# A state-space convolution in front of two gated feed-forward layers: the first quarter prepared in another order

## The chip, the core and the metric

One Trainium2 chip, one core. The time is the device time of one execution in microseconds. The kernel before was run three times: 1150.04, 1151.3 and 1151.69 us, median 1151.3 us. The profile is of a fourth execution.

## The reference

`x` is 64 rows of 32 heads by 512 positions, float32. All of it is computed in one launch:

```python
K = 2.0 * einsum('hn,hnl->hl', Ct, exp(dtA[:, :, None] * arange(512))).real   # a 512-tap filter for each of 32 heads
y = causal_convolution(x, K) + x * D[:, None]        # written with an FFT of length 1024
y = y * (arange(512) < length[batch])                # a mask by the length of the row
x1 = x + FFN0(y)        # w2(silu(w1 y) * (w3 y)), width 1792, weights scaled by blocks of 128 x 128
x2 = x1 + FFN1(x1)      # width 1376, with a low-rank term per batch row, gathered by index
out = x2 + gelu(BitLinear(x2))      # RMS norm, 8-bit activations, ternary weights
```

The filter needs, for each head, sines, cosines and powers of 64 complex numbers; `K` comes out of small products of two tables, S (16 coarse steps) and Fm (32 fine steps).

## The kernel before

**Tiling.** The 32 heads are worked in four quarters of eight (`NT`, `HPT`), 512 tokens each (64 rows by 8 heads). A quarter is at once a tile of the first feed-forward layer. Products are fp32 in three passes: each operand is split into a rounded high part and a low remainder, and `mm3` (lines 137 to 139) issues high x high, high x low and low x high. The high part is always written by ScalarE (a copy with rounding), the low part by VectorE (a subtraction that needs the high part).

**A filter on its way to TensorE.** For quarter t: `angles(t)` makes the arguments of the sines in `theta`, four operations on 128 x 512, in place, by GpSimd; `sines(t)` on ScalarE fills one of two `trig` buffers; `magnitudes(t)` on GpSimd fills one of two `mag` buffers by nine doublings, once VectorE has the powers `pw`; `state_tables(t)` on VectorE makes S, Fm and a small term `dm` for `D`; `state_sums(t)` on TensorE makes the filter in a PSUM bank `pk`; `kernel_high(t)` and `kernel_low(t)` split it; SP writes both halves to DRAM rows (`kernel_rows`) and reads them back as Toeplitz blocks (`toeplitz`), 128 shifted copies of each row, in four pairs of heads, two loads of 512 KB for each pair (high and low).

**Convolution and chunk.** `conv(t)` multiplies for each pair q the Toeplitz blocks with x, 24 products of 64 to 256 columns, in turn into two PSUM banks; VectorE masks (line 1298), ScalarE rounds (`conv_high`), VectorE subtracts (`low_half`, line 1288). The result stands where x stood in `a_hi`, `a_lo` and is the input of the feed-forward layer. `chunk(c)` is two blocks of 128 hidden units for all four tiles: for each tile twelve gate and twelve up products of 512 columns for block 0, the same for block 1, then 24 down products. In chunk 0 the convolution of tile t + 1 is put between up and down products of tile t. The up products of block 1 reuse the bank that the silu of block 0 has read (`pe.wait_ge(s_silu[0], m + 1)`).

**Order.** Each engine has its instructions written out in order, and semaphores tie the engines together. Nothing is reordered: an instruction that waits holds all behind it on its engine, DMA issues on SP too. ScalarE's order in the front is: two small sines, `sines(0)`, `x_high(0)`, `sines(1)`, `kernel_high(0)`, `sines(2)`, `kernel_high(1)`, `sines(3)`, first weights, `conv_high(0)`, `x_high(1)`, chunk 0. VectorE: `exp32` for the step sizes (14 operations), the step itself, `exp32` for the powers (a multiplication and 14 operations on 128 x 288), coefficients, `state_tables` 0 and 1, `kernel_low(0)`, `x_low(0)`, `kernel_low(1)`, the mask, scaling of the first weights (line 1271), `masked(0)` with the low halves of these weights (`first_weights`) after pairs 0 and 1, `x_low(1)`, `state_tables` 2 and 3, chunk 0. GpSimd: `angles(0)`, four small ones for `den`, `angles(1)`, `magnitudes` 0 and 1, then `angles` and `magnitudes` of 2 and of 3, masks and an identity. A `link` makes the next VectorE (or GpSimd) instruction wait for the end of the one before. TensorE: `state_sums` 0 and 1, `conv(0)`, chunk 0 with `state_sums` 2 and 3 ahead of `conv(1)`. SP: parameters (three loads), x tile 0 and small inputs, first weights, zeros, `kernel_rows(0)`, `toeplitz(0)`, x tile 1, `kernel_rows(1)`, `toeplitz(1)` (each pair waits until `conv(0)` has read the buffer), x tiles 2 and 3, weights, indices, quarters 2 and 3.

## Time and profile before

| | us |
|---|---|
| median of three runs | 1151.3 |
| profiled execution, its own time | 1152.8 |
| its span, first to last instruction | 1150.9 |
| TensorE in products | 1067.7 (93%) |
| TensorE loading weights | 900.1 (78%) |
| VectorE | 548.8 (48%) |
| ScalarE | 302.9 (26%) |
| GpSimd | 154.8 (13%) |

The engines' busy shares by slices of 1/40 of the span, 28.8 us each, in tenths; PEclk is the granted clock of TensorE:

```
PE   0799999999999999999889999999999999988774
DVE  7544554334344444344763343443443343357786
ACT  1222221211212121211441121122132131124675
POOL 7800000000000000000141001001010010023425
PEclk9999999999999999999999999999999999998897
DMA  2775310010101000020311022021021021032103
```

TensorE does nothing of weight in the first slice, is filled from the third on, and thins out in the last four. GpSimd is busy only in the first two slices. The granted clock is written as a share of 2.4 GHz; where it is 0.5, the array runs at 1.2 GHz. PE is TensorE, PEld its weight loads, DVE VectorE, ACT ScalarE, POOL GpSimd, SPq the queue on which SP issues DMAs.

### The profile page before, as it was taken

Reading aid. Unit: us, or ns where it says so; the run is one execution under the profiler, and the core shown is the slowest. Engines: PE = TensorE matmul, PEld = TensorE weight load, DVE = VectorE, ACT = ScalarE, POOL = GpSimd, SP = SyncE. Lnnn points to the kernel's source line nnn. Section 1 sums busy time; section 2 is a strip of 40 time slices with the busy share of each in tenths; the row PEclk is TensorE's granted clock in tenths of the full one; section 3 lists DMA queues with packets and bytes.
Section 4 is the critical chain, followed back from the end, with each engine's and each line's share of the span. In section 5 each row is a group of like instructions: output and inputs, shape, how many; then the busy total and the mean of one; then the engine's idle time right before and its main releaser. Section 6 shows DMA issues by size and latency. Waiting matters only on the chain.

```text
span 1150.9 us, 13707 instructions
## 1 busy us (share of the span) xinstructions
PE 1067.7 (93%) x5431; PEld 900.1 (78%) x5434; DVE 548.8 (48%) x661; ACT 302.9 (26%) x485; POOL 154.8 (13%) x194
## 2 busy tenths in 40 slices
PE   0799999999999999999889999999999999988774
PEld 0679888888888888888778888888888888876651
DVE  7544554334344444344763343443443343357786
ACT  1222221211212121211441121122132131124675
POOL 7800000000000000000141001001010010023425
PEclk9999999999999999999999999999999999998897
DMA  2775310010101000020311022021021021032103
GB/s 100 236 247 197 111 41 16 1 55 0 55 0 55 0 15 39 0 92 1 128 65 54 30 68 68 27 82 55 27 84 53 27 97 39 27 110 74 47 1 146
DMA packets 26655, 73.92 MB, mean 64 GB/s; under 512 B 5442, under 2 KB 5634, under 8 KB 26498
## 3 DMA queue, kind: packets, MB, share of 16 engines
q1 hardware_dynamic: 20994, 48.35, 12.0%
q0 software_dynamic: 5632, 25.17, 7.1%
q8 instruction: 19, 0.31, 0.1%
q14 instruction: 10, 0.08, 0.0%
HBM read 69.15 MB, written 4.36 MB: 64 GB/s over the span
## 4 chain that ended last, share of the span: by engine, by line
PE 84%; DVE 5%; POOL 4%; issue 3%; ACT 2%; DMA 1%; SPq 0%; DVEq 0%; ACTq 0%; POOLq 0%
PE ps_gu L137 18%; PE ps_gu L138 18%; PE ps_gu L139 18%; PE ps_d L137 8%; PE ps_d L138 8%; PE ps_d L139 8%; PE ps_t L139 1%; PE ps_t L138 1%; PE ps_t L137 1%; POOL theta L435 1%; POOL mag L435 1%; DMA lr_raw<-in_tab_l,rows 1%; PE ps_gu L836 1%; PE ps_t L727 1%; POOL trig L431 1%
## 5 line engine op out<-in xcount | busy, mean ns | idle before, releaser
L137 PE MATMUL ps_gu<-a_hi,gu_hi 128*128 128x512 f32 x800 | 316.4, 396 | 2.2 <-DVE a_lo L1288 2.2
L138 PE MATMUL ps_gu<-a_lo,gu_hi 128*128 128x512 f32 x800 | 313.9, 392 | 0.0
L139 PE MATMUL ps_gu<-a_hi,gu_lo 128*128 128x512 f32 x800 | 313.1, 391 | 0.0
L139 PEld LDWEIGHTS ps_gu<-a_hi,gu_lo 128*128 128x128 f32 x800 | 151.2, 189 | 32.5
L137 PEld LDWEIGHTS ps_gu<-a_hi,gu_hi 128*128 128x128 f32 x800 | 151.9, 190 | 31.5 <-DVE a_lo L1288 2.3
L138 PEld LDWEIGHTS ps_gu<-a_lo,gu_hi 128*128 128x128 f32 x800 | 151.8, 190 | 28.6
L1425 DVE TENSOR_TENSOR s_act<-s_act,ps_gu 128x512 f32<-128x512 f32 x44 | 30.2, 687 | 194.7 <-PE ps_gu L139 194.6
L1318 DVE TENSOR_TENSOR s_act<-s_act,ps_gu 128x512 f32<-128x512 f32 x56 | 38.5, 687 | 152.8 <-PE ps_gu L139 152.8
L307 POOL DMA_INDIRECT lr_raw<-in_tab_l,rows x48 | 46.0, 959 | 369.3 <-PE ps_t L727 345.4
L137 PE MATMUL ps_d<-h_hi,dn_hi 128*128 128x512 f32 x224 | 87.6, 391 | 0.0
L139 PE MATMUL ps_d<-h_hi,dn_lo 128*128 128x512 f32 x224 | 87.2, 389 | 0.0
L138 PE MATMUL ps_d<-h_lo,dn_hi 128*128 128x512 f32 x224 | 87.2, 389 | 0.0
L932 ACT ACTIVATE s_act<-ps_gu 128x512 f32<-128x512 f32 x56 | 33.5, 598 | 183.5 <-PE ps_gu L139 183.4
L1364 DVE TENSOR_TENSOR acc<-acc,ps_d 128x2048 f32<-128x2048 f32 x24 | 54.9, 2287 | 48.5 <-PE ps_d L139 48.4
L936 ACT ACTIVATE h_hi<-s_act 128x512 fp32r<-128x512 f32 x56 | 35.4, 632 | 158.2 <-DVE s_act L1318 158.2
L307 POOL DMA_INDIRECT ar_raw<-in_tab_a,rows x8 | 8.1, 1016 | 489.9 <-PE ps_d L139 409.2
L1005 ACT ACTIVATE s_act<-ps_gu 128x512 f32<-128x512 f32 x44 | 26.3, 598 | 176.8 <-PE ps_gu L139 176.8
L137 PE MATMUL ps_d<-dn_hi,h_hi 128*128 128x512 f32 x176 | 68.8, 391 | 0.2 <-DVE x1b L1529 0.2
L138 PE MATMUL ps_d<-dn_lo,h_hi 128*128 128x512 f32 x176 | 68.7, 391 | 0.0
L139 PE MATMUL ps_d<-dn_hi,h_lo 128*128 128x512 f32 x176 | 68.5, 389 | 0.0
L1011 ACT ACTIVATE h_hi<-s_act 128x512 fp32r<-128x512 f32 x44 | 27.8, 631 | 151.3 <-DVE s_act L1425 149.9
L1471 DVE TENSOR_TENSOR x1b<-x1b,ps_d 128x2048 f32<-128x2048 f32 x20 | 45.7, 2287 | 36.3 <-PE ps_d L139 36.3
(239 smaller groups left out, 1727.6 us busy)
## 6 DMA issues: line engine op xcount, KB each, us to landing
raw<-in_w SPq DMA_DIRECT2D x26, 768.0 KB, 5.7
toep_hi<-krev_hi SPq DMA_DIRECT2D x16, 512.0 KB, 5.9
toep_lo<-krev_lo SPq DMA_DIRECT2D x16, 512.0 KB, 6.9
acc<-in_x_t SPq DMA_DIRECT2D x4, 1024.0 KB, 10.1
out<-x1b SPq DMA_DIRECT2D x16, 256.0 KB, 2.0
w_all<-in_wq SPq DMA_DIRECT2D x1, 1024.0 KB, 8.3
raw<-in_wq SPq DMA_DIRECT2D x4, 256.0 KB, 4.3
lr_raw<-in_tab_l,rows POOLq DMA_INDIRECT x48, 4.1
```

The lines of the kernel that those rows point to most:

```text
L137: pe.matmul(out_ap, st_hi, mv_hi, start=start, stop=False, skip_group_check=skip)
L138: pe.matmul(out_ap, st_hi, mv_lo, start=False, stop=False, skip_group_check=skip)
L139: return pe.matmul(out_ap, st_lo, mv_hi, start=False, stop=stop, skip_group_check=skip)
L307: return pool.indirect_dma_start(out=dst, out_offset=None, in_=table, in_offset=bass.IndirectOffsetOnAxis(ap=group, axis=0))
L932: act.activation(s_act[:, f], ps_gu[G_BANK[f]], ACT.Silu).then_inc(s_silu[f], 1)
L936: act.activation(h_hi[:, f], s_act[:, f], ACT.Copy).then_inc(s_hh[f], 1)
L1005: act.activation(s_act[:, f], ps_gu[G_BANK[f]], ACT.Silu).then_inc(s_silu[f], 1)
L1011: act.activation(h_hi[:, f], s_act[:, f], ACT.Copy).then_inc(s_hh[f], 1)
L1318: dve.tensor_tensor(s_act[:, f], s_act[:, f], ps_gu[U_BANK[f]], ALU.mult).then_inc(s_mul[f], 1)
L1364: dve.tensor_tensor(x_tile(acc, t), x_tile(acc, t), ps_d[:], ALU.add).then_inc(s_ev, 1)
L1425: dve.tensor_tensor(s_act[:, f], s_act[:, f], ps_gu[U_BANK[f]], ALU.mult).then_inc(s_mul[f], 1)
L1471: dve.tensor_tensor(zt, zt, ps_d[:], ALU.add).then_inc(s_ev, 1)
```

## The change

- **Angles.** `angles(t)` moves from GpSimd to VectorE. `angles(0)` stands ahead of the powers, `angles(1)` behind `state_tables(0)` and `x_low(0)`, `angles(2)`, `x_low(1)` and `angles(3)` behind all of the first convolution's work, ahead of `state_tables` 2 and 3. GpSimd keeps the magnitudes, now in one row. The argument of the angles (`turns`) and the powers have places of their own.
- **Parameters.** The load of the step sizes and decays is issued first, and `exp32` waits for it alone.
- **First Toeplitz rows.** The filter of quarter 0 is copied unsplit (`k_f`), written once and loaded once, four loads of 512 KB in place of eight; ScalarE rounds each pair of heads on chip and VectorE subtracts in place (`first_toeplitz_low`), 128 x 1024 each. Loads of the later quarters are as before.
- **State sums.** Those of quarter 1 stand before pair 2 of `conv(0)`, those of quarters 2 and 3 before pairs 2 and 3 of `conv(1)`, and the halves of these filters are made between the masks of that convolution.
- **Filling products.** Fourteen products of 512 columns on `a_hi` stand before `conv(0)`, once the filter of quarter 0 has landed in DRAM. They write a PSUM bank that nobody reads before it is written anew.
- **ScalarE and VectorE** have their work of the front in another order, written out in the diff; `sines(2)` and `sines(3)` now stand between `x_high(1)` and the first silu.

Line numbers of the diff are those of the listing above; indentation is cut and "..." marks what is left out.

```diff
@@ -40,6 +40,7 @@
+BUSY = 14
@@ -311,9 +315,9 @@
-    sp.dma_start(e3[:, 2], par[:, 2]).then_inc(s_par, 16)
...
-    sp.dma_start(par_sb[:, 2:4], par[:, 3:5]).then_inc(s_par, 16)
+    sp.dma_start(e3[:, 2], par[:, 2]).then_inc(s_par2, 16)
+    sp.dma_start(par_sb[:, 2:4], par[:, 3:5]).then_inc(s_par2, 16)
@@ -329,23 +333,31 @@
-            sp.wait_ge(s_half, t + 1)
+            sp.wait_ge(s_half, t)
...
+    def first_toeplitz():
+        sp.wait_ge(s_kf, 1)
+        sp.dma_start(krev[0][0:HPT, 0:L].rearrange("h (a b) -> a h b", b=NB), k_f[:]).then_inc(s_kw[0], 16)
+        sp.wait_ge(s_kw[0], 16)
+        sp.wait_ge(s_kz, 32)
+        for q in range(4):
+            sp.dma_start(toep_lo[:, 2 * q:2 * q + 2].bitcast(F32),
+                         bass.AP(tensor=krev[0].tensor, offset=2 * q * KROW,
+                                 ap=[[1, P], [KROW, 2], [1, L]])).then_inc(s_T[q], 16)
...
-            if t:
-                sp.wait_ge(s_conv, 4 * (t - 1) + q + 1)
+            sp.wait_ge(s_conv, 4 * (t - 1) + q + 1)
...
-    kernel_rows(0)
-    sp.wait_ge(s_kz, 32)
-    toeplitz(0)
+    first_toeplitz()
@@ -427,28 +439,11 @@
-    def ts(o, i, a, b, op0, op1=None):
-        link(pool.tensor_scalar(o, i, a, b, op0, op1) if op1 is not None
-             else pool.tensor_scalar(o, i, a, 0.0, op0, ALU.add))
...
-    r0, den, d2 = sm[3][:], sm[4][:], sm[5][:]
-    def angles(t):
-        hs = slice(t * HPT, (t + 1) * HPT)
-        if t:
-            pool.wait_ge(s_trig, t)
-        if t >= 2:
-            pool.wait_ge(s_sf, 3 * (t - 1))
-        rnd = trig[:, t % 2]
-        tt(theta[:], bc(r0[:, hs], 2, 64), bc(lgrid[:], 1, HPT), ALU.mult)
-        tt(theta[:], theta[:], bc(shift[:], 1, HPT), ALU.add)
-        ts(rnd, theta[:], MAGIC, MAGIC, ALU.add, ALU.subtract)
-        pool.tensor_tensor(theta[:], theta[:], rnd, ALU.subtract).then_inc(s_theta, 1)
+    den, d2 = sm[4][:], sm[5][:]
@@ -465,17 +460,12 @@
-    angles(0)
...
-    angles(1)
...
-    magnitudes(0)
-    magnitudes(1)
-    for t in range(2, NT):
-        angles(t)
+    for t in range(NT):
@@ -585,12 +575,26 @@
+    def busy_array():
+        pe.wait_ge(s_xh, 1)
+        pe.wait_ge(s_kw[0], 16)
+        for k in range(BUSY):
+            pe.matmul(ps_gu[0], a_hi[:, k % KB, 0:P], a_hi[:, k % KB, 0:TT], start=True, stop=True)
...
-            pe.wait_ge(s_T[q], 32 * (t + 1))
+            if t == 0 and q == 2:
+                state_sums(1)
+            if t == 1 and q >= 2:
+                state_sums(q)
+            if t:
+                pe.wait_ge(s_T[q], 32 * t + 16)
+            else:
+                pe.wait_ge(s_tl, q + 1)
@@ -630,13 +634,10 @@
                 last.then_inc(s_u[f], 1)
-            if first and t == 0:
-                for n in range(2, NT):
-                    state_sums(n)
             if first and t + 1 < NT:
...
             if first and t == 0:
-                pe.wait_ge(s_kl, NT)
+                pe.wait_ge(s_kl, NT - 1)
             for f in range(2):
@@ -665,7 +666,7 @@
     state_sums(0)
-    state_sums(1)
+    busy_array()
     conv(0)
@@ -893,34 +894,37 @@
         act.wait_ge(s_kp, t + 1)
-        if t >= 2:
-            act.wait_ge(s_kw[t - 2], 32)
+        if t == 3:
+            act.wait_ge(s_kw[1], 32)
         act.activation(k_hi[:, t % 2], pk[:, t], ACT.Copy).then_inc(s_kh, 1)
+    def conv_high(t, pairs=(0, 1, 2, 3)):
+        for q in pairs:
+            h0 = t * HPT + 2 * q
+            act.wait_ge(s_cmul, 4 * t + q + 1)
+            act.activation(a_hi4[:, :, h0:h0 + 2].rearrange("p k h b -> p h k b"),
+                           ytmp[:, q % 2].rearrange("p h (k b) -> p h k b", k=KB), ACT.Copy).then_inc(s_yhi, 1)
...
     sines(1)
-    kernel_high(0)
-    sines(2)
-    kernel_high(1)
-    sines(3)
+    act.wait_ge(s_kp, 1)
+    act.activation(k_f[:], pk[:, 0], ACT.Copy).then_inc(s_kf, 1)
     for f in range(2):
...
                        raw[:, f, 0:2].rearrange("p a n -> p (a n)"), ACT.Copy).then_inc(s_whg[f], 1)
+        for q in (2 * f, 2 * f + 1):
+            act.wait_ge(s_T[q], 16)
+            act.activation(toep_hi[:, 2 * q:2 * q + 2], toep_lo[:, 2 * q:2 * q + 2].bitcast(F32),
+                           ACT.Copy).then_inc(s_th, 1)
         act.activation(dn_hi[:, f], raw[:, f, 2], ACT.Copy).then_inc(s_whd[f], 1)
-    def conv_high(t):
-        for q in range(4):
-            h0 = t * HPT + 2 * q
-            act.wait_ge(s_cmul, 4 * t + q + 1)
-            act.activation(a_hi4[:, :, h0:h0 + 2].rearrange("p k h b -> p h k b"),
-                           ytmp[:, q % 2].rearrange("p h (k b) -> p h k b", k=KB), ACT.Copy).then_inc(s_yhi, 1)
-    conv_high(0)
+    conv_high(0, (0,))
+    kernel_high(1)
+    conv_high(0, (1, 2, 3))
     x_high(1)
-    act.wait_ge(s_mag, NT)
+    sines(2)
+    sines(3)
@@ -943,9 +947,12 @@
+                conv_high(1, (0,))
...
+                conv_high(1, (1,))
...
-            if first and t + 1 < NT:
+                conv_high(1, (2, 3))
+            elif first and t + 1 < NT:
@@ -1186,18 +1193,36 @@
-    dve.wait_ge(s_par, 48)
+    dve.wait_ge(s_par, 16)
...
-    ar, ai, ut, r0, den, d2, em, t0 = (t[:] for t in sm)
+    ar, ai, ut, _, den, d2, em, t0 = (t[:] for t in sm)
+    r0 = turns[:]
...
+    dve.wait_ge(s_par2, 32)
...
+    def angles(t):
+        hs = slice(t * HPT, (t + 1) * HPT)
+        rnd = trig[:, t % 2]
+        if t:
+            dve.wait_ge(s_trig, t)
+        if t >= 2:
+            dve.wait_ge(s_sf, 3 * (t - 1))
+        tt(theta[:], bc(r0[:, hs], 2, 64), bc(lgrid[:], 1, HPT), ALU.mult)
+        tt(theta[:], theta[:], bc(shift[:], 1, HPT), ALU.add)
+        ts(rnd, theta[:], MAGIC, MAGIC, ALU.add, ALU.subtract)
+        dve.tensor_tensor(theta[:], theta[:], rnd, ALU.subtract).then_inc(s_theta, 1)
...
+    dve.wait_ge(s_plink, 2)
+    dve.wait_ge(s_step, 1)
+    angles(0)
@@ -1240,9 +1265,9 @@
-        dve.wait_ge(s_kh, t + 1)
-        if t >= 2:
-            dve.wait_ge(s_kw[t - 2], 32)
+        dve.wait_ge(s_kh, t)
+        if t == 3:
+            dve.wait_ge(s_kw[1], 32)
@@ -1253,29 +1278,28 @@
-    state_tables(0)
-    state_tables(1)
-    kernel_low(0)
-    x_low(0)
-    kernel_low(1)
-    dve.wait_ge(s_len, 16)
-    link(dve.tensor_copy(len_f[:], len_i[:]))
-    dve.wait_ge(s_grid, 3)
-    link(dve.tensor_tensor(cmask[:], pos[:], bc(len_f[:], 1, KB), ALU.is_lt))
-    dve.wait_ge(s_sc0, 16)
-    for f in range(2):
+    def first_scale(f):
...
-    def first_weights(f):
+    def first_toeplitz_low(q):
+        dve.wait_ge(s_th, q + 1)
+        pair = toep_lo[:, 2 * q:2 * q + 2]
+        dve.tensor_tensor(pair, pair.bitcast(F32), toep_hi[:, 2 * q:2 * q + 2].bitcast(F32),
+                          ALU.subtract).then_inc(s_tl, 1)
+    def first_gate_up_low(f):
...
+    def first_down_low(f):
@@ -1288,19 +1312,24 @@
+    def mask(t, q):
+        j = 4 * t + q
+        dve.wait_ge(s_conv, j + 1)
+        if j >= 2:
+            dve.wait_ge(s_yhi, j - 1)
+            dve.wait_ge(s_ylo, j - 1)
+        dve.tensor_tensor(ytmp[:, q % 2], conv_bank[q % 2].rearrange("p (i n) -> p i n", i=2),
+                          bc(cmask[:].rearrange("p k b -> p (k b)"), 1, 2), ALU.mult).then_inc(s_cmul, 1)
...
-            dve.wait_ge(s_conv, 4 * t + q + 1)
-            if 4 * t + q >= 2:
-                dve.wait_ge(s_yhi, 4 * t + q - 1)
-                dve.wait_ge(s_ylo, 4 * t + q - 1)
-            dve.tensor_tensor(ytmp[:, q % 2], conv_bank[q % 2].rearrange("p (i n) -> p i n", i=2),
-                              bc(cmask[:].rearrange("p k b -> p (k b)"), 1, 2), ALU.mult).then_inc(s_cmul, 1)
+            mask(t, q)
...
-            if t == 0 and q < 2:
-                first_weights(q)
+            if t == 1 and q in (1, 2):
+                kernel_low(q + 1)
@@ -1326,9 +1355,6 @@
-            if first and t == 0:
-                kernel_low(2)
-                kernel_low(3)
@@ -1368,8 +1394,37 @@
-    masked(0)
+    state_tables(0)
+    x_low(0)
+    angles(1)
+    dve.wait_ge(s_len, 16)
+    link(dve.tensor_copy(len_f[:], len_i[:]))
+    dve.wait_ge(s_grid, 3)
+    link(dve.tensor_tensor(cmask[:], pos[:], bc(len_f[:], 1, KB), ALU.is_lt))
+    dve.wait_ge(s_sc0, 16)
+    first_scale(0)
+    first_toeplitz_low(0)
+    state_tables(1)
+    first_toeplitz_low(1)
+    first_scale(1)
+    first_gate_up_low(0)
+    mask(0, 0)
+    first_toeplitz_low(2)
+    mask(0, 1)
+    first_toeplitz_low(3)
+    low_half(0, 0)
+    kernel_low(1)
+    first_gate_up_low(1)
+    mask(0, 2)
+    low_half(0, 1)
+    mask(0, 3)
+    low_half(0, 2)
+    low_half(0, 3)
+    for f in range(2):
+        first_down_low(f)
+    angles(2)
...
+    angles(3)
...
```

## Rows read from the trace of the kernel before

**Rows 1.** The page, the chain that ended last: shares of the span by engine.

```profile
PE 84%; DVE 5%; POOL 4%; issue 3%; ACT 2%; DMA 1%; SPq 0%; DVEq 0%; ACTq 0%; POOLq 0%
```

**Rows 2.** Waits of TensorE, 0 to 130 us: total us, times, longest us.

```profile
PE ps_d L582 <- DVE Fm L1239: 28.9, 2, 27.1
PE ps_t L137 <- DMA toep_lo<-krev_lo: 5.6, 1, 5.6
```

**Rows 3.** Timeline, 0 to 60 us: start, duration, engine, line, operation, tiles, [idle before].

```profile
3.50 0.20 DVE L1165 TENSOR_SCALAR tmp<-par_sb 128x64 f32<-128x64 f32 x1 [3.50 <-DMA par_sb<-in_par]
...
7.96 1.30 DVE L1169 TENSOR_TENSOR pin<-sm,pow 128x288 f32<-128x288 f32 x1
...
11.28 0.31 DVE L1166 TENSOR_SCALAR tmp<-tmp 128x288 f32<-128x288 f32 x1
...
19.22 0.46 DVE L1172 SCALAR_TENSOR_TENSOR pw<-tmp,kint 128x288 f32<-128x288 f32 x1
...
21.87 3.25 POOL L435 TENSOR_TENSOR mag<-mag,pw 128x8 f32<-128x8 f32 x9
...
25.11 0.62 DVE L1169 TENSOR_TENSOR S<-coef,trig 128x128 f32<-128x128 f32 x2
...
29.14 0.37 ACT L898 ACTIVATE k_hi<-ps_d 16x256 fp32r<-16x256 f32 x1 [6.79 <-PE ps_d L584]
...
32.75 0.39 SPq L342 DMA_DIRECT2D toep_hi<-krev_hi  x1
...
38.46 0.55 PE L137 MATMUL ps_t<-a_hi,toep_hi 128*128 128x256 f32 x1 [5.62 <-DMA toep_lo<-krev_lo]
```

**Rows 4.** DMA issues, 28 to 33 us: size, median us from issue to landing.

```profile
krev_lo<-k_lo SPq DMA_DIRECT2D x1, 16.0 KB, 1.5
```

**Rows 5.** Loads of toep_hi, 28 to 52 us.

```profile
DMA to landing us min/median/max: 3.7/6.4/10.0
```

**Rows 6.** VectorE by shape, 0 to 80 us: busy us, mean ns | idle before.

```profile
L1251 DVE TENSOR_TENSOR a_lo<-acc,a_hi 128x2048 fp32r<-128x2048 f32 x2 | 4.6, 2282 | 1.1 <-ACT a_hi L891 1.1
L1271 DVE TENSOR_TENSOR raw<-raw,scale 128x1536 f32<-128x1536 f32 x2 | 3.4, 1763 | 0.0
L1288 DVE TENSOR_TENSOR a_lo<-ytmp,a_hi 128x512 fp32r<-128x512 f32 x4 | 2.8, 688 | 0.1
L1276 DVE TENSOR_TENSOR gu_lo<-raw,gu_hi 128x1024 fp32r<-128x1024 f32 x2 | 2.5, 1251 | 7.0 <-ACT gu_hi L909 7.0
```

**Rows 7.** ScalarE by shape, 0 to 80 us.

```profile
L909 ACT ACTIVATE gu_hi<-raw 128x1024 fp32r<-128x1024 f32 x2 | 2.1, 1040 | 0.0
...
L932 ACT ACT_TABLE_LOAD x1 | 1.3, 1283 | 4.4 <-PE ps_gu L139 4.4
```

**Rows 8.** Timeline, 60 to 140 us.

```profile
61.66 0.80 PE L137 MATMUL ps_gu<-a_hi,gu_hi 128*128 128x512 f32 x1 [2.17 <-DVE a_lo L1288]
...
66.89 0.39 PE L137 MATMUL ps_gu<-a_hi,gu_hi 128*128 128x512 f32 x1
...
77.34 0.39 PE L137 MATMUL ps_t<-a_hi,toep_hi 128*128 128x256 f32 x1
...
80.08 0.37 PE L137 MATMUL ps_gu<-a_hi,toep_hi 128*128 128x256 f32 x1
```

**Rows 9.** Windows, TensorE: us, busy (products), granted clock, DMA share, GB/s.

```profile
38.50:59.00 20.50, 20.32 (x95) 1.00 0.83 283
1037.36:1045.36 8.00, 8.00 (x33) 0.65 0.21 66
...
1093.91:1101.91 8.00, 6.53 (x37) 0.79 0.00 0
```

**Rows 10.** Timeline of TensorE, 1020 to 1151 us.

```profile
1050.72 0.50 PE L137 MATMUL ps_d<-gu_hi,h_hi 128*128 128x512 f32 x1 [2.67 <-DVE h_lo L1571]
...
1093.91 0.56 PE L137 MATMUL ps_d<-gu_hi,h_hi 128*128 128x512 f32 x1 [2.83 <-DVE h_lo L1571]
```

More of the change, by code:

```diff
@@ L103, in build @@
             pin = sb("pin", [P, 9, HEADS])
-            pw = sb("pw", [P, 9, HEADS])
             tmp = [sb(f"tmp{i}", [P, 9 * HEADS]) for i in range(4)]
@@ L145, in build @@
         s_par, s_drow, s_len, s_ix, s_rb, s_id = (sem(n) for n in ("s_par", "s_drow", "s_len", "s_ix", "s_rb", "s_id"))
+        s_par2, s_kf, s_th, s_tl = (sem(n) for n in ("s_par2", "s_kf", "s_th", "s_tl"))
         r_row, r_next = sem("r_row"), sem("r_next")
@@ L201, in build @@
             coef = [sb(f"coef{i}", [P, HEADS]) for i in range(2)]
+            turns = sb("turns", [P, HEADS])
+            pw = sb("pw", [P, 9, HEADS])
+            k_f = sb("k_f", [NA, HPT, NB])
             drow = sb("drow", [1, HEADS])
@@ L877, in _ @@
                 act.wait_ge(s_step, 1)
-                act.activation(trig_small[0], sm[3][:], ACT.Sin, scale=TWO_PI).then_inc(s_sin, 1)
-                act.activation(trig_small[1], sm[3][:], ACT.Sin, scale=TWO_PI / 2).then_inc(s_sin, 1)
+                act.activation(trig_small[0], turns[:], ACT.Sin, scale=TWO_PI).then_inc(s_sin, 1)
+                act.activation(trig_small[1], turns[:], ACT.Sin, scale=TWO_PI / 2).then_inc(s_sin, 1)
                 def sines(t):
```

## The prediction

> **What bounds the kernel now.** I read the page's shares of the ending chain first: TensorE holds 84% of it, so a change counts only by what it takes out of TensorE's own sequence or out of the time before that sequence closes up [rows 1]. Second, TensorE's waits in the first 130 us: 27.1 us until the first state tables, 5.6 us for Toeplitz rows [rows 2], and 2.17 us before the first gate product [rows 8]. All of the change lies there; behind 62 us the order of TensorE's work is only rearranged by a few microseconds and I let it shift as a block. Third, the timeline of the first 60 us, for the path that ends these waits: parameters at 3.50, powers of the decay written by 19.7, tables from 25.11, kernel rows rounded at 29.14, first Toeplitz DMA issued at 32.75, first convolution product at 38.46 [rows 3].
>
> Fourth, the clock. Convolution products run from 38.5 to 59 at 20.32/95 = 0.214 us each [rows 9], in the next quarter at (80.08 - 77.34)/24 = 0.114 us [rows 8]. The first twelve gate products take 5.23 us from 61.66 to 66.89, 0.436 each, and the one at 66.89 is the first short one [rows 8]. The granted clock reads 1.00 in the front all the same, while a later stretch of 8 us with the same slow start reads 0.65: 1.2 GHz for 0.35 x 2 x 8 = 5.6 us, then 2.4 [rows 9]. I read the front column as not yet recording and go by the spacing: everything before 66.7 is at 1.2 GHz, as the products there are spaced, though TensorE was in products without a break from 38.5 to 59. Dense 512-column products bring the rise (5.0 and 5.6 us after their start, 3.4 in a third place [rows 9]), the convolution's mix of short ones does not; once risen, the mix keeps it. So the change is worth what it does to the start of the chunk and to the clock of 96 convolution products.
>
> **Start to first Toeplitz row.** The first vector work, at 3.50 [rows 3], now waits for the first of three loads instead of the last: a gain between nothing and half of the 3.50; I take 0.8, an estimate. Angles for quarter 0 go on VectorE ahead of the powers: three operations of two tensors at 0.69 (L1288 has their size [rows 6]) and one scalar operation, between 0.31 (288 columns [rows 3]) and 0.69, I take 0.45; with the links 2.5 us. The powers then run without GpSimd beside them: before, 7.96 to 19.68 = 11.7 us, with the first multiplication at 1.30 [rows 3]. Alone, 10 operations at 0.46 + 0.03 and 5 at 0.31 + 0.03 are 6.6 us (bounds 6.6 and 11.7; the two rows at 0.46 and 0.31 are what they cost with GpSimd quiet). Powers at 16.3 instead of 19.7. GpSimd's nine multiplications, 3.25 us, then end near 19.9, before they are wanted at 21.5. Coefficients lay between 19.68 and 25.11 [rows 3]; one of them stood against GpSimd, I take 4.4 for 5.4. Tables from 20.7, kernel sums ready 4.0 later as before (25.11 to 29.14): 24.7. Of the 4.0 the last 2.0 are the sums, as TensorE waited until 27.1 [rows 2].
>
> Now comes a new wait. ScalarE has the second sines ahead of the rounding of the kernel row, VectorE has x_low(0) (2.28 [rows 6]) and four angle operations (2.5) behind the tables that end at 22.5. The sines finish at 28.0 rather than when the sums are ready at 24.7, and the copy k_f ends at 28.4. One DMA write instead of two and no low half: 1.5 us for such a write [rows 4]; I take 1.7, between 1.5 and 2.2, rows issued at 30.1 against 32.75. Both x_low(0) and the angles now run beside GpSimd's magnitudes, nine operations in 3.25 us [rows 3]. Between nothing and one of these, 0.36 us, in front of each of five vector operations is 0 to 1.8 us; I take 0.5: issue at 30.6. The page "SBUF — State Buffer" of the Trainium skill (section "SBUF: two separate sides") says that a VectorE operation with two SBUF inputs and a GpSimd operation that reads SBUF take one port pair by exclusive lock, the loser waiting for a whole instruction. The rows agree where they show it (1.30 against 0.46 above), and by the rule all five would wait. That is the rule that speaks against this change: by it the rows are issued at 31.9 and the time is 1.3 us above mine.
>
> Of the Toeplitz loads the quickest landed 3.7 us after its issue and the slowest 10.0 [rows 5]. That is 6.3/7 = 0.9 between neighbours beside the 0.5 between their issues (0.39 for one [rows 3] and a gap), so four loads land at 34.3, 35.7, 37.1, 38.5. ScalarE rounds one in 1.04, VectorE subtracts in 1.25 [rows 7, 6]: convolution pair 0 at 36.7 against 38.46.
>
> **Filling products.** They start when the kernel row has landed, 30.6, and 14 at 0.43 are 6.0 us: over by 36.6, just before pair 0, so they cost nothing; each microsecond by which the Toeplitz rows came sooner, or the kernel row later, would show as loss, up to the whole 6.0. If the rise comes 3.4 to 5.6 us after their start it comes inside them. Value: pairs at 2.74 instead of 5.13.
>
> **Convolution of quarter 0, warm.** Now VectorE paces it, with the table of quarter 1 and the second scaling in its queue. From pair 0 at 36.7: tables(1) 1.7 (they lie in the 2.0 between 25.11 and 27.1), low(1) 1.25, pair 1 at 39.6; scaling 1.76, gate low 1.25, mask 0.69, low(2) 1.25 (ScalarE's gate rounding 1.04 and rounding of pairs 2 and 3 lie under it but for 0.3), mask, low(3) 1.25 [rows 6, 7]. Pair 2 starts at 44.6, pair 3 follows at 47.3 and ends at 50.2; mask, rounding and low half cost 2.17 as before [rows 8]: gate products at 52.4 against 61.66, gain 9.3. The state sums of quarter 1 (half of 2.0 at the fast clock) fall into the 2.3 us hole between pairs 1 and 2. SP's loads for quarter 1 wait for kernel_low(1), behind low(3) and a low half on VectorE: out at 47.5, written at 49, eight loads landed by 63, wanted from 66. The x tiles and weights behind them on SP, 3.5 MB at 283 GB/s [rows 9], land by 76, and none is wanted before 80.
>
> **First chunk.** Twelve warm products take 2.9, not 5.2: 2.3 more. Against that stands a second new wait. The first silu must come before the fourth product group, at 52.4 + 8.3 = 60.7. ScalarE has sines(2) and sines(3) ahead of it, these wait for VectorE: two down lows at 0.69, angles 2.5, x_low(1) 2.28, angles 2.5; then sine 0.6 (half of 1.04 for 1024 columns, and a start), table load 1.28 [rows 7], silu 0.6: 52.4 + 11.1 = 63.5. TensorE stands 2.8 us. Bounds: 0 if the sums above are 2.8 too long, 4 if each operation meets one more delay. In the kernel before ScalarE waited for the gate product before that load, with products running, so it cost nothing. State sums 2 and 3 change place, 2.2 us either way; their kernel_high and kernel_low sit between masks and need nothing on time.
>
> **Sum.** 9.3 + 2.3 - 2.8 = 8.8 us. The profiled execution took 1152.8 with a span of 1150.9; the median of three is 1151.3, and the difference is taken off that: **1142.5**.
>
> **The clock in the new holes.** A hole of 2.67 us left TensorE at 2.4 GHz, one of 2.83 us was followed by a slow stretch of 0.21 x 2 x 8 = 3.4 us [rows 9, 10]. The silu hole is 2.8 by launch and 2.6 by records, on that edge. If the clock falls there, the fourth group runs slow and the rise comes within it or just behind it: 1.7 to 3.4 us more, inside my likeliest case. The page "TensorE: Matmul & The Clock Gate" of the Trainium skill (section "Why this matters for your kernels") allows holes up to about 3 us between bursts, by which this hole is harmless and the sum stays 8.8; the row with 2.83 us goes against it, so I don't rely on it.
>
> **Rivals.** (A) *The filling does not raise the clock.* For it: the rise needed up to 5.6 us, and the filling offers 6.0 with a gap behind it; 20 us of convolution did not raise it. Against it: all three known rises fit in. Then pairs stay at 5.13: end of pair 3 at 36.7 + 4 x 5.13 + 2.1 for the sums = 59.3, against 61.66 - 2.17 = 59.5, chunk slow start as before, silu late by about 0.5: **1151.3** within 1. (B) *The clock rises and falls in the 2.3 us before pair 2*, where only state sums run. Two pairs at 5.13 cost 4.8, the slow start of the chunk is then hidden in the silu hole: **1147.3**. For it: the convolution mix is thin on both sides. Against: 2.3 is below 2.67. (C) *Slower:* the silu hole drops the clock and the fourth group is too short to bring it back (12 x 0.427 = 5.1 us, known rises 3.4 to 5.6), so the convolution of quarter 1 runs slow as quarter 0 did: 12 x 0.2 + 96 x 0.1 + 2 for the sums + 2.4 in the down products = 16.4. 1142.5 + 16.4 = **1158.9**. It decides as soon as the hole passes 2.7 to 2.8 and the rise takes over 5.1 us. (D) *Port conflicts eat the front:* the full 1.8 instead of 0.5 and powers at 9 us instead of 6.6 give 1146, still faster.
>
> **Chances.** Likeliest case 0.67 (own range 1139.5 to 1146.5, with D), B 0.10, A 0.13, C 0.07, others 0.03. The range from 1139 to 1149.5 holds the first two and the near edge of others; it leaves out A and C. A measurement can tell about 0.2%, 2.3 us, from no change. Faster 0.80, within 0.2% 0.12, slower 0.08.
>
> **What would show it.** k_f's copy right behind the second sines near 28.5 and not behind the sums; products of 0.23 us spacing by the end of the filling; convolution pairs of 2.74; first gate product near 52.4 with 0.23 spacing from the start; a hole near 60.7 to 63.5 ended by silu; the whole order of TensorE 8.8 earlier from the first down product on. The forecast is wrong if the filling ends at 0.43, if pairs 2 and 3 start more than 2 us off, or if slow products follow the hole at 60.7 for more than 4 us.

## The result, and the profile after

The changed kernel takes 1146.72 us (median of 14 runs, 1142.74 to 1151.06) against 1151.59 for the kernel before (14 runs, 1150.04 to 1153.90): a ratio of 0.995, interval 0.9938 to 0.9962. The forecast was 1142.5 with a range of 1139 to 1149.5. The profiled run took 1143.93 us with a span of 1142.1, that is 8.9 less than the profiled run of before (1152.82).

The 14 runs are not one heap. Six lie between 1142.7 and 1143.9 with a mean granted clock of 0.984 to 0.987; six between 1147.7 and 1148.9 with 0.977 or 0.978; one stands between them (1145.7, 0.983) and one above (1151.1, 0.975). The kernel before shows no such groups in its 14 runs. So the median of 1146.7 stands in a gap between two groups, and the profile is of the quicker one. What makes the other is a question of its own below.

The shares of the ending chain in the page of after, against [rows 1]; the waits of TensorE from 0 to 130 us (total, times, longest), against [rows 2]:

```profile
PE 84%; DVE 8%; ACT 3%; issue 2%; DMA 2%; POOL 1%; DVEq 0%; ACTq 0%; POOLq 0%
```

```profile
PE ps_d L572 <- DVE Fm L1264: 23.2, 1, 23.2
PE ps_gu L583 <- DMA krev_hi<-k_f: 5.2, 1, 5.2
PE ps_gu L137 <- ACT s_act L936: 2.6, 1, 2.6
PE ps_gu L137 <- DVE a_lo L1312: 2.2, 1, 2.2
PE ps_t L137 <- DVE toep_lo L1291: 2.2, 2, 1.3
```

The timeline of after from 0 to 90 us (start, duration, engine, line, operation, tiles, [idle before]), against [rows 3, 8]:

```profile
2.56 0.20 DVE L1172 TENSOR_SCALAR tmp<-par_sb 128x64 f32<-128x64 f32 x1 [2.56 <-DMA par_sb<-in_par]
...
15.74 0.46 DVE L1179 SCALAR_TENSOR_TENSOR pw<-tmp,kint 128x288 f32<-128x288 f32 x1
...
16.56 3.16 POOL L443 TENSOR_TENSOR mag<-mag,pw 128x8 f32<-128x8 f32 x9
...
20.11 5.93 POOL L443 TENSOR_TENSOR mag<-mag,pw 128x8 f32<-128x8 f32 x9
...
22.67 0.41 DVE L1264 TENSOR_TENSOR Fm<-trig,mag 128x256 f32<-128x256 f32 x1
23.00 2.27 DVE L1276 TENSOR_TENSOR a_lo<-acc,a_hi 128x2048 fp32r<-128x2048 f32 x1
...
28.36 0.36 ACT L912 ACTIVATE k_f<-ps_d 16x256 f32<-16x256 f32 x1
...
30.29 1.92 SPq L346 DMA_DIRECT2D toep_lo<-krev_hi  x4
...
30.40 5.06 PE L583 MATMUL ps_gu<-a_hi 128*128 128x512 f32 x14 [5.21 <-DMA krev_hi<-k_f]
...
36.74 0.36 PE L137 MATMUL ps_t<-a_hi,toep_hi 128*128 128x256 f32 x1 [1.28 <-DVE toep_lo L1291]
...
44.32 0.39 PE L137 MATMUL ps_t<-a_hi,toep_hi 128*128 128x256 f32 x1 [0.89 <-DVE toep_lo L1291]
...
52.13 0.50 PE L137 MATMUL ps_gu<-a_hi,gu_hi 128*128 128x512 f32 x1 [2.17 <-DVE a_lo L1312]
...
61.19 1.28 ACT L936 ACT_TABLE_LOAD   x1
62.48 0.60 ACT L936 ACTIVATE s_act<-ps_gu 128x512 f32<-128x512 f32 x1
...
63.13 0.50 PE L137 MATMUL ps_gu<-a_hi,gu_hi 128*128 128x512 f32 x1 [2.57 <-ACT s_act L936]
...
86.58 2.29 DVE L1390 TENSOR_TENSOR acc<-acc,ps_d 128x2048 f32<-128x2048 f32 x1
```

Windows of TensorE in after (us, busy and products, granted clock, DMA share, GB/s), against [rows 9]. The record of the clock starts with its first change, so 1.00 ahead of that says nothing; in the last two rows it does:

```profile
36.74:39.45 2.71, 2.71 (x24) 1.00 1.06 404
...
63.13:64.50 1.37, 1.36 (x6) 1.00 1.05 386
64.50:68.00 3.50, 3.50 (x12) 0.51 1.07 403
```

What the reader is to see: the fourteen fill products take 5.06 us where fourteen at 0.43 would take 6.0, so the clock rises inside them; a convolution pair then takes 2.71 instead of 5.13, and the gate products start at 52.13 instead of 61.66 [rows 8]. Behind the hole of 2.57 us that the silu leaves, the clock is at 1.2 GHz for 3.5 us. One landmark holds the whole front together, the first accumulation on VectorE: 86.58 here, and in the kernel before

```profile
94.01 2.29 DVE L1364 TENSOR_TENSOR acc<-acc,ps_d 128x2048 f32<-128x2048 f32 x1
```

so 7.4 of the 8.9 us come from ahead of it, and 1.5 from slow stretches further on that lie elsewhere from run to run: in the trace of before the granted clock is 0.50 from 561.8 to 565.1 us with 17 products, in that of after it is 1.00 there.

### The profile page after: what moved, and what is told of

Its sections match the earlier page's. It is cut to its first block, busy times and chain, and to the rows that moved or that the text cites. A ratio compares the mean times of both kernels' runs of the same rounds, so it can differ in the third digit from the quotient of the medians.

```text
span 1142.1 us, 13740 instructions
## 1 busy us (share of the span) xinstructions
PE 1059.2 (93%) x5448; PEld 891.6 (78%) x5448; DVE 556.2 (49%) x680; ACT 306.7 (27%) x489; POOL 135.7 (12%) x178
## 4 chain that ended last, share of the span: by engine, by line
PE 84%; DVE 8%; ACT 3%; issue 2%; DMA 2%; POOL 1%; DVEq 0%; ACTq 0%; POOLq 0%
PE ps_gu L137 18%; PE ps_gu L138 18%; PE ps_gu L139 18%; PE ps_d L137 8%; PE ps_d L138 8%; PE ps_d L139 8%; PE ps_t L139 1%; PE ps_t L137 1%; PE ps_t L138 1%; DMA lr_raw<-in_tab_l,rows 1%; PE ps_gu L837 1%; PE ps_t L728 1%; DVE ar_lo L1443 1%; DVE z_new L1576 1%; ACT a_hi L1001 1%
## 5 line engine op out<-in xcount | busy, mean ns | idle before, releaser
L1018 ACT ACTIVATE h_hi<-s_act 128x512 fp32r<-128x512 f32 x44 | 27.8, 631 | 151.6 <-DVE s_act L1480 150.2
```

Source lines behind the costliest of these rows:

```text
L1018: act.activation(h_hi[:, f], s_act[:, f], ACT.Copy).then_inc(s_hh[f], 1)
```

## The experiments

The theory: the gain is the clock's, raised by the filling and kept by the convolution; the rearranged front only makes room for it. The rivals: the front's own microseconds count; the filling is needed in part only; the second group of runs comes from somewhere else than the front.

| kernel | median us (runs) | ratio to before, interval | first gate product | first accumulation |
|---|---|---|---|---|
| before | 1151.6 (14) | | 61.66 | 94.01 |
| after | 1146.7 (14) | 0.995, 0.9938 to 0.9962 | 52.13 | 86.58 |
| after again | 1144.3 (6) | 0.994, 0.9921 to 0.996 | 51.90 | 84.78 |
| after, third time | 1143.8 (5) | 0.9933, 0.992 to 0.9947 | 52.24 | 86.70 |
| no filling | 1152.2 (12) | 1.0003, 0.9994 to 1.0013 | 61.44 | 94.33 |
| 8 fill products | 1152.8 (11) | 1.0006, 0.9996 to 1.0015 | 61.41 | 94.32 |
| filling alone | 1152.1 (11) | 1.0002, 0.9992 to 1.0011 | 61.67 | 93.65 |
| ScalarE queue alone | 1151.6 (11) | 0.9998, 0.9989 to 1.0007 | 61.44 | 92.78 |
| filling and ScalarE queue | 1143.4 (5) | 0.9923, 0.9909 to 0.9937 | 54.41 | 85.72 |
| bridged hole | 1143.2 (6) | 0.9925, 0.9909 to 0.994 | 51.78 | 84.68 |
| silu sooner | 1146.4 (6) | 0.9946, 0.9925 to 0.9968 | 56.01 | 87.48 |
| reordered | 1138.2 (4) | 0.9875, 0.986 to 0.989 | 50.27 | 81.92 |
| reordered again | 1139.7 (5) | 0.9898, 0.9883 to 0.9914 | 50.49 | 81.21 |
| reordered and bridged | 1139.9 (4) | 0.9887, 0.9872 to 0.9902 | 50.25 | 80.93 |

Each ratio is to the kernel before as it ran beside that kernel (medians 1151.6 to 1152.2 us). Both repeats, no filling, the bridged hole, silu sooner and "reordered again" ran on one chip (number 9), the other experiments on another (number 6). The last two columns are of the profiled run alone. One run of the filling alone took 6057 us, for no reason that a trace shows; the medians don't feel it.

**The same kernel again, twice.** No edit.

> The changed kernel once more, for the spread of its runs and for a second trace. So far its runs fall into two groups, about 1143.4 and 1148.3 us, with one at 1151, and the profiled one is of the first group: there the clock rose within the filling products and stayed up through the first convolution. Theory: in the slower group the clock falls in the hole between convolution pairs 1 and 2 (only state sums there), pairs 2 and 3 run at 5.1 us instead of 2.7, and the gate products start near 57 instead of 52.1. Rival: in the slower group the filling products do not raise the clock at all; then all four pairs run at 5.1 us and the time is 1151. Rival: the clock falls only in the hole before the first silu and stays down through the second convolution; that would cost 10 us and more, and the runs would stand at 1153 or above. Expected: median between 1143 and 1148.5, both groups present.

> The changed kernel once more, for its second group of runs. Of 20 runs so far 11 lay at 1142.6 to 1145.7 with a mean clock of 0.983 to 0.988, nine at 1147.7 to 1151.1 with 0.975 to 0.978. If the second group is the clock fallen in the hole before pair 2, any profile with a mean of 0.978 shows pairs 2 and 3 at 5.1 and gate products near 56.3, and every run with 0.978 lies 4.5 to 5 us above those with 0.985; a profile with 0.985 shows them at 2.74 and 52.1. If it is something else (falls in the tail), the front is the same in both.

The runs of the first repeat: 1142.6, 1143.9, 1142.6, 1144.6 (clock 0.984 to 0.988) and 1147.9, 1148.1 (0.978). Of the second: 1142.6 to 1143.8 three times, 1145.2 and 1145.8 with 0.981 and 0.979. Over all 25 runs of this kernel nine lie at 1147.7 or above. On this chip it is two in 11, and five runs in a row without one. No profile fell into that group, so the last expectation was not decided for it; its other half held, the profile with 0.987 shows the gate products at 52.24. The first repeat's profile shows another fall, behind the hole ahead of the gate products:

```profile
51.90:53.00 1.10, 1.10 (x5) 1.00 1.01 268
53.00:57.00 4.00, 4.00 (x12) 0.57 1.03 347
57.00:61.00 4.00, 4.00 (x19) 1.00 1.05 401
```

It costs nothing: the silu comes when ScalarE is through, and TensorE then waits 0.95 us for it instead of 2.57. In that trace the clock is then spared behind the silu hole, and the first accumulation comes at 84.78.

**No filling.** The call of `busy_array` removed.

```
                 state_sums(0)
-                busy_array()
                 conv(0)
```

> The changed kernel without the fourteen filling products. If the clock is what the change gains, all four pairs of the first convolution run slow (5.1 us each), gate products start near 61.5 as in the kernel before, the wait for the first silu shrinks to about 0.5 us, and the time is 1151 to 1152, equal to the kernel before. If the rearranged front itself gained, it would be 1149 or less.

TensorE's rows of that kernel:

```profile
36.54 0.55 PE L137 MATMUL ps_t<-a_hi,toep_hi 128*128 128x256 f32 x1 [11.48 <-DVE toep_lo L1290]
46.90 1.03 PE L572 MATMUL ps_d<-dm,onehot 1*16 1x256 f32 x2
...
61.44 0.80 PE L137 MATMUL ps_gu<-a_hi,gu_hi 128*128 128x512 f32 x1 [2.17 <-DVE a_lo L1311]
```

Pair 0 starts 1.9 us sooner than before [rows 3], two pairs take 10.36 us as before, the state sums between them eat the 1.9 (2.0 us at the slow clock), and the gate products start where they always did. The rearranged front without the clock is worth nothing.

**Eight fill products.** `BUSY = 8`.

> The changed kernel with 8 filling products instead of 14: they end near 33.8, and TensorE stands some 2.9 us before pair 0. If the rise needs the filling up to pair 0, all four pairs run at 5.13 and the time is 1151 to 1152, as without filling. If 3.4 us are enough and the gap does no harm, 1143 to 1144. If it is a matter of where the rise happens to fall, runs of one kernel scatter between 1143 and 1152, and the median lies between.

```profile
PE ps_t L137 <- DVE toep_lo L1291: 2.7, 1, 2.7
```

```profile
36.92:38.00 1.08, 1.08 (x7) 0.72 1.06 412
38.00:59.20 21.20, 21.20 (x109) 0.50 0.46 144
```

First the wait ahead of pair 0, then two windows. In this trace the clock did rise, since a fall is recorded in pair 0: the rise is lost behind a hole of 2.7 us ahead of the convolution, and the convolution didn't bring it back in 21 us. None of eleven runs was below 1151.1. Eight of them have a mean clock of 0.971 to 0.974, three have 0.986, the value of the kernel before, whose front is not in the record: in these three the filling probably raised nothing; they took 1152.4 to 1153.4. Fourteen products, with a hole of 1.28 behind them, kept it: here the filling had to come closer to the convolution.

**The filling alone**, in the kernel before, with nothing rearranged.

```
+                def busy_array():
+
+                    pe.wait_ge(s_xh, 1)
+                    pe.wait_ge(s_kw[0], 32)
+                    for k in range(BUSY):
+                        pe.matmul(ps_gu[0], a_hi[:, k % KB, 0:P], a_hi[:, k % KB, 0:TT], start=True, stop=True)
...
                 state_sums(1)
+                busy_array()
                 conv(0)
```

> The kernel before with the fourteen filling products alone, between the state sums of quarter 1 and pair 0, released when both kernel rows of quarter 0 have landed; nothing of the front is rearranged. If the gain is the clock's alone: fill from about 32.5 to 38.5, pair 0 at 38.6, four pairs at 2.74 without the split on VectorE between them, gate products near 51.8 instead of 61.66, warm from the start, 1140 to 1144, as good as the whole change. If the rearranged front is needed for it (the 1.9 us by which pair 0 comes sooner, and the sums in another place), 1145 to 1148. If the clock doesn't rise here, 1151.6.

Neither of the first two came: the clock rose (fourteen products in 4.60 us), and yet nothing was gained. The timeline of that kernel, four engines:

```profile
38.60 0.36 PE L138 MATMUL ps_t<-a_hi,toep_hi 128*128 128x256 f32 x1 [1.21 <-DMA toep_lo<-krev_lo]
...
48.65 1.26 POOL L452 TENSOR_TENSOR theta<-theta,trig 128x512 f32<-128x512 f32 x1
...
49.95 0.63 ACT L895 ACTIVATE trig<-theta 128x512 f32<-128x512 f32 x1 [11.20 <-POOL theta L452]
50.48 1.04 ACT L918 ACTIVATE gu_hi<-raw 128x1024 fp32r<-128x1024 f32 x1
...
51.55 1.28 DVE L1285 TENSOR_TENSOR gu_lo<-raw,gu_hi 128x1024 fp32r<-128x1024 f32 x1 [7.52 <-ACT gu_hi L918]
...
53.37 0.68 DVE L1307 TENSOR_TENSOR ytmp<-ps_gu,cmask 128x512 f32<-128x512 f32 x1
...
54.20 0.55 PE L138 MATMUL ps_gu<-a_hi,toep_hi 128*128 128x256 f32 x1 [6.76 <-DVE ytmp L1307]
```

```profile
54.20:59.30 5.10, 5.10 (x24) 0.50 1.02 308
```

Read it upwards from the last product, the first of pair 3 (the expectation of the next experiment calls it pair 2): TensorE waits for a bank that the mask has to empty; the mask stands in VectorE's queue behind the low half of the weights; that waits for ScalarE's rounding; and that stands in ScalarE's queue behind the sines of quarter 3, whose angles GpSimd delivers at 49.9. The kernel before has the same chain (its VectorE idles 7.0 us for `gu_hi` [rows 6]), but there slow products cover it, and the same product comes at the same time behind a wait of 0.18 us:

```profile
54.19 0.55 PE L137 MATMUL ps_gu<-a_hi,toep_hi 128*128 128x256 f32 x1 [0.18 <-DVE ytmp L1298]
```

With quick products it becomes a hole of 6.8 us, and behind the hole pair 3 runs at the slow clock.

**ScalarE's queue, with and without the filling.** Everything else as in the kernel before:

```
                 kernel_high(0)
-                sines(2)
                 kernel_high(1)
-                sines(3)
                 for f in range(2):
...
+                sines(2)
                 conv_high(0)
                 x_high(1)
+                sines(3)
                 act.wait_ge(s_mag, NT)
```

> The kernel before with two edits: the fourteen filling products, and on ScalarE the roundings of kernel row 1 and of the weights ahead of the sines of quarters 2 and 3, which wait for GpSimd. Nothing else of the front is rearranged. In the trace of the filling alone the clock rose, but ScalarE stood for the angles of quarter 3 until 49.95 with the weight rounding queued behind it, VectorE stood behind that rounding with the masks of pairs 1 to 3 behind it, and TensorE stood 6.8 us before pair 2. If that queue is the whole reason why the filling alone gave nothing: pair 0 at 38.6, no hole above 1 us until the convolution ends near 49.8, gate products near 51.9 to 52.5, no silu hole (sines of quarter 3 are done by 53), first accumulation at 82 to 83 instead of 94.0, total 1139.5 to 1142: better than the changed kernel. If the rest of the rearranged front is needed as well (GpSimd's share, split on chip), 1145 or more.

> The kernel before with the reordered ScalarE queue and without filling. By both theories no gain: the convolution of quarter 0 stays at 5.13 per pair (no dense products before it) and sets the gate products near 61.5; 1151 to 1152. If it gains over 1 us, ScalarE's queue cost time on its own in the kernel before, and part of any gain of the two edits together is that.

The order alone gives nothing, the filling alone nothing, both together 8.7 us by their medians: as much as the quicker group of the changed kernel, with the front left alone. The total was 1.4 us above the upper end that I had given, the gate products 1.9 later. Rows of its timeline and a window show by what:

```profile
45.96 2.31 DVE L1285 TENSOR_TENSOR gu_lo<-raw,gu_hi 128x1024 fp32r<-128x1024 f32 x1
...
48.55 0.38 PE L138 MATMUL ps_gu<-a_hi,toep_hi 128*128 128x256 f32 x1 [1.11 <-DMA toep_lo<-krev_lo]
...
52.26 0.69 DVE L1307 TENSOR_TENSOR ytmp<-ps_gu,cmask 128x512 f32<-128x512 f32 x1 [1.78 <-PE ps_gu L140]
```

```profile
50.50:57.00 6.50, 4.31 (x16) 0.50 0.70 203
```

The loads of the last pair (two halves per pair, eight loads) landed 1.1 us late, and behind the late load the clock fell in the middle of pair 3. VectorE's low half took 2.31 instead of 1.25 beside GpSimd's angle operations, but that cost nothing here: VectorE then stood 1.78 us for TensorE before the last mask. In the changed kernel, with single loads and no angles on GpSimd, the gate products come 2.3 us sooner, and the silu hole that it opens takes 2.6 back. Which of its edits removes the late load was not tried.

**The hole ahead of pair 2, bridged.** Behind the state sums, in the changed kernel:

```
                         if t == 0 and q == 2:
                             state_sums(1)
+                            pe.wait_ge(s_whg[0], 1)
+                            for k in range(4):
+                                pe.matmul(ps_gu[0], gu_hi[:, 0, 0, k], gu_hi[:, 0, 1].rearrange("p k n -> p (k n)"),
+                                          start=True, stop=True)
```

> The changed kernel with four more 512-column products on the first gate weights between the state sums of quarter 1 and convolution pair 2 (0.9 us, the length of the idle time there). If the hole between pairs 1 and 2 is what splits the runs, the slower group goes and the median falls to 1143.5 with a spread of 1.5 us. If the filling products are what fails in the slow runs, or if the silu hole is, the slower group stays at its share of a half near 1148.3 and the median does not move by more than chance.

```profile
51.78 0.79 PE L137 MATMUL ps_gu<-a_hi,gu_hi 128*128 128x512 f32 x1 [2.17 <-DVE a_lo L1316]
```

The pairs stay where they were, and the highest of six runs is 1145.72: 1143.2 against 1144.3 for the changed kernel on the same chip. The spread is 4.6 us and not the 1.5 expected. With nine runs in 25 in the changed kernel's upper group, six below it in a row would come by luck 7 times in 100 (0.64 to the sixth); with the two in 11 of this chip, 30 times in 100, and the unchanged kernel had five such runs in a row itself. So this hints at the hole and shows nothing. Its profile holds the clock through the pairs and loses it behind the hole ahead of the gate products, as the first repeat's does: the first of them took 0.79 us, where it takes 0.50 at the full clock.

**The silu sooner.** In VectorE's queue the angles of quarter 2 go ahead of the low halves of the down weights, and `x_low(1)` behind the angles of quarter 3.

```
                 low_half(0, 3)
+                angles(2)
                 for f in range(2):
                     first_down_low(f)
-                angles(2)
-                x_low(1)
                 angles(3)
+                x_low(1)
```

> The changed kernel with VectorE's order behind the first convolution changed to angles(2), the two down lows, angles(3), x_low(1). The first silu should come near 61.0 instead of 63.1, the hole before the fourth product group shrink from 2.6 to 0.5 us. The sum says 2.1 us less in the faster group (1141.3), and where the clock fell in that hole, a further 1 to 2. If the slower group comes from the hole between pairs 1 and 2, it stays, at about 1148: the cold start of the chunk is then no longer hidden. If it comes from the silu hole, it goes and all runs stand at 1141.

The silu no longer stands in the list of waits, but the median is no better than the changed kernel's. Its profile is the one in which the convolution loses the clock. Windows and a product of TensorE:

```profile
36.76:44.00 7.24, 6.71 (x66) 1.00 0.57 213
44.35:46.00 1.65, 1.65 (x13) 0.84 0.00 0
46.00:58.00 12.00, 9.83 (x42) 0.50 0.74 226
```

```profile
44.35 0.39 PE L137 MATMUL ps_t<-a_hi,toep_hi 128*128 128x256 f32 x1 [0.88 <-DVE toep_lo L1291]
...
56.01 0.80 PE L137 MATMUL ps_gu<-a_hi,gu_hi 128*128 128x512 f32 x1 [2.17 <-DVE a_lo L1312]
```

Pairs 0 and 1 are warm, pair 2 turns cold about 1.2 us behind its start, pair 3 is cold, and the gate products start 3.9 us later than in after. This is rival B of the prediction; this run took 1145.15. Three other runs of this kernel lie at 1147.7 to 1148.5 with 0.978. The quick ones (1143.0, 1143.1) are no quicker than the changed kernel's, where 1141.3 was expected. Perhaps a fall ahead of the gate products is no longer hidden behind the silu; no trace of a quick run shows it.

**Reordered.** If VectorE's queue makes the hole ahead of pair 2 and the silu hole, both should go by order alone: state sums of quarter 1 under the landing of the Toeplitz rows, both weight scalings and the first weight split before the Toeplitz halves arrive, the splits of pairs 0 to 2 ahead of the first mask.

```
                 busy_array()
+                state_sums(1)
                 conv(0)
...
                 first_scale(0)
+                first_scale(1)
+                first_gate_up_low(0)
+                state_tables(1)
                 first_toeplitz_low(0)
-                state_tables(1)
                 first_toeplitz_low(1)
-                first_scale(1)
-                first_gate_up_low(0)
+                first_toeplitz_low(2)
                 mask(0, 0)
...
```

with ScalarE's roundings in the same order, the down weights behind the first rounding of the convolution, and the order of "silu sooner" behind them. Then the same with nine products in the hole of 2.17 us ahead of the gate products.

> The changed kernel reordered: state sums of quarter 1 under the landing of the Toeplitz rows, the split of all four pairs ahead of the mask, the rounded kernel row and the weight splits on VectorE, down lows before the last angles. By my account of the trace (VectorE paces the convolution): no hole between pairs 1 and 2, pairs at 2.74 end at 47.6, gate products at 49.8 instead of 52.1, silu hole 0.5 us; sum 2.4 + 1.5 us under the better runs of the changed kernel, 1139.5 to 1140.5, and no runs near 1148, as the hole where the clock fell is gone. Rival (the time of the chunk is bound by what follows, the loads of quarter 1 or its tables): 1142 to 1143, gain taken back before 75. Rival (the clock falls in the 2.2 us hole before the gate products, which the silu hole no longer hides): 2 to 3 us more in part of the runs.

> As the reordered kernel, with nine products of 512 columns from the rounded gate weights in the hole of 2.2 us before the first gate product. If the clock falls in that hole in part of the runs, these are gone and the median is 1139 to 1140 with all runs within 1.5 us; if it doesn't matter, the same as the reordered kernel within 0.5 us.

> The reordered kernel once more, beside the changed kernel on the same chip. By the same account its hole before pair 2 is gone, so it has no second group: all runs within 1136.5 to 1139.5, a ratio of 0.987 to 0.989 to the kernel before. If the second group comes from elsewhere, about 9 in 20 of its runs lie 4 to 5 us higher, at 1142 to 1144.

TensorE in the reordered kernel:

```profile
37.01:48.00 10.99, 10.99 (x99) 1.00 0.62 207
50.27:52.00 1.73, 1.73 (x7) 0.95 1.03 295
52.00:55.00 3.00, 3.00 (x8) 0.50 1.05 402
```

The four pairs run without a hole in 10.9 us. The clock still falls behind the hole of 2.17 us ahead of the gate products in this trace, which was the last rival of the expectation; in the repeat's profile it holds there. The gate products start 1.9 sooner than in after, the first accumulation comes at 81.92. The median of 1138.2 lies 1.3 under my range, and this is the best of all kernels here: 13.8 us under the kernel before on its chip. Repeated on another, it gave 1139.7, with five runs from 1138.3 to 1142.8: no run 4 to 5 us above the rest in the first four, one in the second five (1142.8, clock 0.981). So my statement that it has no second group failed by that run, and three of the five lie above the 1139.5 that I had given as the end; over 13 runs of reordered kernels it is one, where the changed kernel has nine in 25 (such a difference comes by luck about 6 times in 100). With the bridge the fall ahead of the gate products is gone and the first accumulation comes 1.0 sooner than without, but the total isn't better (1139.9), and its four runs lie 3.1 us apart and not 1.5: its trace has more slow stretches behind 1075 us. What decides those is open.

## Why the prediction was right, step by step

**The front up to pair 0** came within 0.6 us everywhere: powers done at 16.2 (16.3 forecast), tables done at 23.1 (22.5), `k_f` copied behind the second sines by 28.7 (28.4), the row written in 1.55 (1.7), Toeplitz rows issued at 30.3 (30.6), filling from 30.4 (30.6), pair 0 at 36.74 (36.7). The sines took the place of the sums as the end of the chain, as said: ScalarE was idle for them until 27.8, with the sums ready by 25.2.

**The port conflicts.** I took 0.5 us for VectorE's five operations beside GpSimd; the rows say none: `x_low(0)` took 2.27 as before (2.28 [rows 6]), the angle operations 0.67 and 0.69. It was GpSimd that lost: its nine multiplications took 3.16 us while VectorE had only short operations, and 5.93 beside the tables and `x_low(0)`. The Trainium skill's page "SBUF — State Buffer" (section "SBUF: two separate sides") gives the port to whichever of the two starts first and has the other wait for the whole instruction. That fits GpSimd here (2.8 us more over nine operations, beside one VectorE operation of 2.27). It doesn't say that VectorE is the one that waits: "all five would wait" and the 1.3 us were my reading of it, and they did not come. Where GpSimd's operations are large, VectorE can pay, as the row of 2.31 us in the experiment shows. Nobody waited for GpSimd here.

**The clock and the convolution** were the term of the sum that mattered, and right: pairs of 2.71 to 2.75 (2.74), pair 2 at 44.32 (44.6), pair 3 at 47.07 (47.3), gate products at 52.13 (52.4), a gain of 9.5 (9.3). The experiments show that rival A's price was right as well (1151.3 forecast, 1152.2 measured without filling).

**The chunk.** Warm first products as forecast (the thirteenth at 54.96, 2.8 us behind the first, where before it stood 5.23 behind [rows 8]); the silu hole 2.57 (2.8). Behind it the clock fell, which I had left between harmless and 3.4 us: it ran slow for 3.5 us and cost 1.6: the second head of quarter 1 starts at 68.85, 5.72 behind the end of the hole, where twelve products at 0.23 and half a pair at 2.74 make 4.13. Rival C did not come: with the fourth group the clock rose again, and from 68.85 the pairs of quarter 1 ran at 2.72 (68.85 to 71.57). The rule of the Trainium skill's page "TensorE: Matmul & The Clock Gate" (section "Why this matters for your kernels"), holes up to about 3 us harmless, is contradicted by this row: 2.57 us, and a fall 1.4 us behind it.

**What the forecast was short of.** The terms gave 8.8, the profiled run 8.9, and that they meet is partly luck. By the rows the terms came to 9.5 + 2.4 - 2.6 = 9.3; the fall behind the silu hole, which the sum put at nothing, took 1.6 of them; of the 7.7 left 7.4 are there at the first accumulation; and 1.5 came from a slow stretch that the profiled run of before happened to have near 562 us. And the median is 4.2 above the forecast, because the likeliest case was made for all runs, and rival B got 0.10. The rivals were set up as alternatives of which one holds for the kernel; the runs show two outcomes of one kernel. Of 25 runs sixteen (1142.6 to 1145.8) lie in the likeliest case's own range and nine in the upper group. The failed step is this: I judged the hole ahead of pair 2 harmless by its length (2.3 us, under a hole of 2.67 that had been harmless once [rows 10]); a hole that had been harmless once showed only that it can be. In the traces the clock fell behind holes of 2.57, 2.71 and 2.17 us, behind one of 1.11, and after the state sums ahead of pair 2; behind the same 2.17 us and the same sums it held in others.

That the 1148 group is rival B in this kernel is likely and not shown. For it: the mechanism stands in the trace of a kernel with the same convolution, and its price was forecast at 4.8 us against 4.6 between the medians of the two groups (1148.1 and 1143.5). The mean clock fits too, by an estimate: 0.978 over a span of 1146 us is 50 us at 1.2 GHz (1146 x 0.022 x 2), against 30 in the traces of after and of the second repeat, 36 in the first repeat's and 46 in that of the silu sooner, the one that lost the clock inside the convolution. A fall behind the silu hole alone adds 3.5. Runs in which the filling raised nothing would be another thing: there the record starts only with the gate products, as in the kernel before, whose mean is 0.986 at 1151 us. Against it: the trace of the silu sooner ran 1145.2, not 1148, and the bridge hints only weakly. No profile of the group itself was caught, so whether the step failed by the hole ahead of pair 2 or by another of the front's holes stays open.

**What the change is worth by parts.** Front without filling: nothing. Filling without the front: nothing. Filling with a free ScalarE queue: all of what the whole change gives in its better runs, with none of five runs in an upper group. So the rest of the rearrangement (angles on VectorE, single loads, split on chip) added nothing to the total that these runs can tell: it moved 2 to 3 us from one hole to another. Only its reordered form was better, by 4 to 5 us (1138.2 and 1139.7); whether the same order does it without the rest was not tried.

## What to carry to other kernels

Products that compute nothing were worth their place here only where they ran close up to the work that was to be warm, and only where nothing behind them opened a long hole: price the fill by the whole stretch it warms, then look for each wait that the slow products used to cover, on every queue that feeds it. A clock that can fall in a hole falls in some runs and not in others: forecast a share of the runs for it and not one outcome, and look at the single runs and their mean clock before the median, bearing in mind that the mean leaves out what lies ahead of the clock's first recorded change. And before a front is rearranged, try the smallest edit that frees the queue: here the filling with two statements moved in ScalarE's order did as much as the filling with all the rest.

## What the runs showed of the hardware that I had not expected

The convolution's short products never raised the clock by themselves (21.2 us at 0.50 in the kernel with eight fill products) and kept it when it was up (four pairs in 10.9 us). GpSimd's nine small operations took 5.93 us against 3.16 beside the tables and a VectorE operation of 2.27 us, which stayed at its time, and GpSimd's 512-column ones stretched a VectorE operation from 1.25 to 2.31. And one and the same kernel lost the clock behind the hole ahead of the gate products in one profile and behind the silu hole in two others, with the first accumulation at 84.78 against 86.58 and 86.70.
